# Last attention block prepares 512 tokens and computes four feed-forward units; the third chunk's transposes stand earlier; one barrier goes

## What is computed

```python
x = layernorm(x + attention(layernorm(x) * gamma + beta, w_qkv))
h = silu(x @ w1.T * s1) * (x @ w2.T * s2)            # 1024 wide
h = gelu(h @ h1.T * h1s); h = gelu(h @ h2.T * h2s)   # 1024 by 1024
out = layernorm(x + (h @ w3.T * s3))
```

## Time and profile before

| what | us |
|---|---|
| median of three runs | 2323.77 |
| the three runs | 2320.99, 2323.77, 2323.83 |
| the profiled execution | 2322.95 |
| its span | 2321.3 |
| TensorE busy | 2286.6 (99%) |
| VectorE busy | 1736.6 (75%) |
| ScalarE busy | 1607.4 (69%) |
| GpSimd busy | 204.5 (9%) |

### The profile page before, as it was taken

How to read it: one execution, slowest core, us unless ns; L and a number is a source line. 1 busy time by engine, 2 the same in 40 slices (tenths; PEclk the granted TensorE clock), 3 DMA queues, 4 the chain that set the end, 5 groups by cost and what they waited for, 6 DMA issues and landing times. The chain is left out here.

```text
span 2321.3 us, 40135 instructions
## 1 busy us (share of the span) xinstructions
PE 2286.6 (99%) x15394; PEld 1406.0 (61%) x15394; DVE 1736.6 (75%) x3755; ACT 1607.4 (69%) x3041; POOL 204.5 (9%) x236
## 2 busy tenths in 40 slices
PE   8999999999999999999999999999899999999998
PEld 4555555555555546555555555554588888888887
DVE  8999998988989887889888889894335544553543
ACT  4677887888989887889888899999523332332332
POOL 3211101011000101000010210001000000000000
PEclk8999999999999999999999999999999999999999
DMA  3110001100000210000021000205400000000000
GB/s 100 30 27 19 1 19 44 33 19 20 19 19 2 58 26 13 19 19 19 1 56 32 22 10 14 74 1 200 148 1 10 1 10 10 10 1 10 10 1 19
DMA packets 38995, 66.48 MB, mean 29 GB/s; under 512 B 9360, under 2 KB 19472, under 8 KB 37392
## 3 DMA queue, kind: packets, MB, share of 16 engines
q1 hardware_dynamic: 35136, 52.35, 8.3%
q0 software_dynamic: 3664, 11.53, 1.5%
HBM read 28.20 MB, written 4.19 MB: 14 GB/s over the span
## 5 line engine op out<-in xcount | busy, mean ns | idle before, releaser
L692 ACT ACTIVATE PR<-bank 128x512 f32<-128x512 f32 (+1 forms) x2176 | 1096.5, 591 | 74.9 <-PE bank L986 68.3
L781 DVE TENSOR_REDUCE pm<-bank 128x1 f32<-128x512 f32 x1471 | 944.0, 683 | 148.8 <-PE bank L960 128.0
L1003 PE MATMUL bank<-PR,V 128*17 128x512 f32 (+3 forms) x4608 | 554.1, 563 | 1.2 <-ACT PR L692 0.9
L1358 PE MATMUL bank<-e_hid,e_h_sb 128*128 128x512 f32 x2048 | 477.6, 395 | 0.0
L981 PE MATMUL bank<-MR,ones 64*128 64x512 f32 (+3 forms) x2304 | 462.9, 384 | 1.1 <-DVE pm L781 0.2
L1358 PEld LDWEIGHTS bank<-e_hid,e_h_sb 128*128 128x128 f32 x2048 | 385.1, 188 | 91.2
L1176 ACT ACTIVATE e_tmp<-bank,e_s_sb 128x512 f32<-128x512 f32 x128 | 88.3, 690 | 341.6 <-PE bank L1358 341.3
L981 PEld LDWEIGHTS bank<-MR,ones 64*128 64x128 f32 x2304 | 236.8, 185 | 72.4 <-ACT PR L692 35.6
L784 DVE CUSTOM_DVE_ANT_0 bank<-bank,below 128x256 f32<-128x256 f32 (+3 forms) x512 | 237.2, 520 | 26.6 <-PE bank L960 25.1
L1299 DVE CAST e_hid<-e_tmp 128x512 fp32r<-128x512 f32 x128 | 54.4, 425 | 258.3 <-ACT e_tmp L1176 258.3
L960 PE MATMUL bank<-KA,QX 64*128 64x512 f32 (+2 forms) x992 | 241.0, 441 | 3.3 <-ACT qk_sb L660 0.6
(11 more groups left out here) (121 smaller groups left out, 1751.2 us busy)
## 6 DMA issues: line engine op xcount, KB each, us to landing
xnT<-in_h_dram SPq DMA_DIRECT2D x8, 1024.0 KB, 5.0
e_h_sb<-in_h_dram POOLq DMA_DIRECT2D x2, 4096.0 KB, 19.9
KA<-qk_hi SPq DMA_DIRECT2D x88, 64.0 KB, 2.3
KA<-qk_lo SPq DMA_DIRECT2D x88, 64.0 KB, 2.2
QX<-qk_hi SPq DMA_DIRECT2D x80, 64.0 KB, 2.3
QX<-qk_lo SPq DMA_DIRECT2D x80, 64.0 KB, 2.3
xres<-in_x_dram SPq DMA_DIRECT2D x8, 512.0 KB, 8.2
out_dram<-e_y SPq DMA_DIRECT2D x7, 512.0 KB, 2.9
```

The lines of the kernel that those rows point to most:

```text
L692: act.activation(PR[:, s % NPB, h, off:QB], ring_bank("score", s, h)[:, off:QB], ACT.Exp).then_inc(exp_done, 1)
L781: dve.reduce_max(pm[:, B % 2, i, a, p, 1 + c:2 + c], bank[:, :], AX.X).then_inc(mx_done, 1)
L1003: last = pe.matmul(ACC[32 * h:32 * h + VW, q:QB], V[:, v_tile(B, tile), GH * (B // NJ % 2) + h, :], PR[:, s % NPB, h, at:at + QB - q], sta ...
L1358: last = pe.matmul(RING[(4 + n) % NR][:, :], w[:, c, P * o:P * (o + 1)], hid[:, (T + layer) % 2, part, c, :], start=(c == 0 and part == 0) ...
```

## The change

In the list of operations: the `norm` of chunk 2 moves ahead of `direct` (1, 2), `maxT` 0 and `direct` (1, 3). In the last block, after step 4 and ahead of the test, a new `x1` lets VectorE compute the statistics, the inverse deviation (by an integer start value and three Newton rounds, in place of ScalarE's root) and the normalised first 512 tokens. After the last scores a new `x1_turn` transposes them and VectorE writes the two parts. After the last block's sums are complete, a `first` unit (4 matmuls, one of the two products of a gate unit) is computed ahead of the accumulator's transposes, and three more after them. These four go to banks 0 to 3, where the feed-forward expects gate units 0 and 1, and its TensorE starts with unit 2. SyncE loads the scales ahead of the weight chunks of the test. ScalarE loads the table of Silu at the end of the attention. The barrier inside the exact branch goes. The first hidden matrix is loaded in two halves of its columns. The kept normalised copy of tile 0's tokens is made at the end of its gate units. The diff, cut to its core:

```diff
@@ -48,6 +48,9 @@
 DEVIATIONS = ((0, 1), (1, 3), (3, NJ))
 WARM = 5
 INTRO_UNITS = 6
+FIRST = 4
+ROOT_BITS = float(0x5F3759DF)
+NEWTON = 3
 COPIED = ("norm", "qk", "v", "maxT", "acc", "acc_copy")
@@ -140,9 +143,10 @@
                 self.ops.append(("av", s - 1))
             self.ops += after.get(s, []) + units[half:] + last.get(s, [])
             if (B, t) == (NB - 1, 4):
-                self.ops.append(("test",))
-        self.ops += [("av", len(STEPS) - 2), ("av", len(STEPS) - 1), ("acc_copy", NB - 1), ("acc", NB - 1),
-                     ("out", NB - 1)]
+                self.ops += [("x1",), ("test",)]
+        self.ops += [("x1_turn",), ("av", len(STEPS) - 2), ("av", len(STEPS) - 1), ("acc_copy", NB - 1),
+                     ("first", 0), ("acc", NB - 1), ("out", NB - 1)]
+        self.ops += [("first", n) for n in range(1, FIRST)]
@@ -181,7 +185,8 @@
 
         def take(use):
             nonlocal now
-            n = min(range(NRING), key=lambda n: back[n])
+            kept = {("acc", NB - 1): FIRST, ("x1_turn", 0): 2, ("x1_turn", 1): 2}.get(use, 0)
+            n = use[1] if use[0] == "first" else min(range(kept, NRING), key=lambda n: back[n])
             now = max(now, back[n] + 105)
             bank[use], former[use], holder[n], back[n] = n, holder[n], use, math.inf
@@ -216,11 +221,14 @@
             if op[0] == "av":
                 width = (QB - offset(*STEPS[op[1]])) / QB
                 now = max(now, ended[op[1]]) + 854 * width + 290
-            if op[0] == "norm":
+            if op[0] in ("norm", "x1_turn"):
                 for f in range(EC):
-                    n = take(("norm", op[1], f))
+                    n = take(op + (f,))
                     now += 440
                     by_scalar(n, now + 195, 730)
+            if op[0] == "first":
+                take(op)
+                now += 910
             if op[0] in LENGTHS:
@@ -240,8 +248,8 @@
                 ("inverse", 1), ("scale", 1), ("scale", 2), ("direct", 0, 0), ("direct", 0, 1), ("norm", 1),
                 ("direct", 0, 2), ("direct", 0, 3), ("stat", 3)]
         ops += first[:half] + [("direct", 1, 0)] + first[half:] + [("rowmax", 0), ("neg", 0)]
-        ops += [("stat", c) for c in range(4, NJ)] + [("direct", 1, 1), ("direct", 1, 2), ("maxT", 0), ("direct", 1, 3),
-                ("norm", 2), ("qk", 2), ("v", 0)] + second + [("inverse", 2)]
+        ops += [("stat", c) for c in range(4, NJ)] + [("direct", 1, 1), ("norm", 2), ("direct", 1, 2), ("maxT", 0),
+                ("direct", 1, 3), ("qk", 2), ("v", 0)] + second + [("inverse", 2)]
         inexact = nc.values_load(low_bits[0:1, 0:1], min_val=0, max_val=2 ** LOW_BITS - 1)
         with nc.If(inexact == 0):
-            nc.all_engine_barrier()
-            feed_forward_exact(nc, w1, s1, w2, s2, h1w, h1s, h2w, h2s, w3, s3, out, xres, ident, eps, banks,
-                               x1T, early, early_load)
+            feed_forward_exact(nc, h1w, h2w, out, xres, ident, eps, banks, x1T, early, early_load, x1_mean, x1_rstd,
+                               scales, w3_scale, first_done)
@@ -529,6 +550,10 @@
                     load_weights(B // NJ + 1)
             sp.wait_ge(v_ready, NU)
             sp.wait_ge(qk_ready, qk_count(NB - 1))
+            for v, scale in enumerate(ff_scales[0:4]):
+                sp.dma_start(scales[:, v, :], scale).then_inc(scale_load, 16)
+            sp.dma_start(w3_scale[:, :], ff_scales[4].rearrange("(o e) -> o e", o=1).broadcast_to([P, E]))\
+              .then_inc(scale_load, 16)
             for n, chunk in enumerate(weight_chunks()):
                 if n == 0:
@@ -538,6 +563,7 @@
                 sp.dma_start(chunks[n % 2], chunk).then_inc(chunk_load[n % 2], 16)
             sp.wait_ge(or_done, n_chunks + 2)
             sp.dma_start(low_row[:, :], low_part[:, :]).then_inc(row_load, 16)
+            sp.wait_ge(scale_load, 16 * 5)
             sp.wait_ge(hi_stacked, stack_count(NB - 1))
             sp.wait_ge(lo_stacked, stack_count(NB - 1))
             for g in range(2, G):
@@ -741,6 +767,7 @@
                     copy_acc(op[1])
                 if op[0] == "acc":
                     copy_sums(op[1])
+            act.activation(table[:, :], eps[:, :], ACT.Silu).then_inc(tabled, 1)
 
         @block.vector
         def _(dve):
...
+            def x1_statistics():
+                dve.wait_ge(res_done, NB - NJ + 1)
+                for i in range(TI):
+                    dve.bn_stats(stats[:, i, :], xres[:, i, :]).then_inc(x1_stat, 1)
+                dve.wait_ge(x1_stat, TI)
+                for i in range(TI):
+                    dve.bn_aggr(x1_mean[:, i, :], stats[:, i, :]).then_inc(x1_stat, 1)
+
+            def x1_inverse():
+
+                value, turn = std[:, 0, :, :], std[:, 1, :, :]
+                dve.wait_ge(x1_stat, 2 * TI)
+                dve.tensor_scalar(value, x1_mean[:, :, 1:2], EPS, None, ALU.add).then_inc(x1_root, 1)
+                dve.wait_ge(x1_root, 1)
+                dve.tensor_scalar(turn.bitcast(int32), value.bitcast(int32), 1, None, ALU.logical_shift_right)\
+                   .then_inc(x1_root, 1)
+                dve.wait_ge(x1_root, 2)
+                dve.tensor_scalar(x1_rstd[:, :, :].bitcast(int32), turn.bitcast(int32), -1.0, ROOT_BITS,
+                                  ALU.mult, ALU.add).then_inc(x1_root, 1)
+                for n in range(NEWTON):
+                    dve.wait_ge(x1_root, 3 * n + 3)
+                    dve.scalar_tensor_tensor(out=turn, in0=x1_rstd[:, :, :], scalar=-0.5, in1=x1_rstd[:, :, :],
+                                             op0=ALU.mult, op1=ALU.mult).then_inc(x1_root, 1)
+                    dve.wait_ge(x1_root, 3 * n + 4)
+                    dve.tensor_tensor(turn, turn, value, ALU.mult).then_inc(x1_root, 1)
+                    dve.wait_ge(x1_root, 3 * n + 5)
+                    dve.scalar_tensor_tensor(out=x1_rstd[:, :, :], in0=turn, scalar=1.5, in1=x1_rstd[:, :, :],
+                                             op0=ALU.add, op1=ALU.mult).then_inc(x1_root, 1)
+
+            def x1_normalise():
+                dve.wait_ge(x1_root, 3 * NEWTON + 3)
+                for i in range(TI):
+                    dve.tensor_scalar(xn_one[:, i, :], xres[:, i, :], x1_mean[:, i, 0:1], x1_rstd[:, i, :],
+                                      ALU.subtract, ALU.mult).then_inc(x1_done, 1)
+
+            def x1T_parts():
+                dve.wait_ge(st_ready, st_count(START[NB - 2] - 1, GH - 1))
+                for f in range(EC):
+                    dve.wait_ge(x1t_ready, f + 1)
+                    dve.tensor_copy(x1T[:, 0, f, :], ring_bank("x1_turn", f)[:, :]).then_inc(x1t_hi, 1)
+                    dve.wait_ge(x1t_hi, f + 1)
+                    dve.tensor_tensor(x1T[:, 1, f, :], ring_bank("x1_turn", f)[:, :], x1T[:, 0, f, :].bitcast(fp32),
+                                      ALU.subtract).then_inc(x1t_lo, 1)
 
             def test_weights():
@@ -868,6 +939,12 @@
                     invert_sums(op[1])
                 if op[0] == "test":
                     test_weights()
+                if op[0] == "x1":
+                    x1_statistics()
+                    x1_inverse()
+                    x1_normalise()
+                if op[0] == "x1_turn":
+                    x1T_parts()
 
         @block.tensor
...
@@ -1004,6 +1083,31 @@
                                          V[:, v_tile(B, tile), GH * (B // NJ % 2) + h, :],
                                          PR[:, s % NPB, h, at:at + QB - q], start=(t == 0), stop=(t == steps_of(B) - 1))
                 last.then_inc(av_done, 1)
+
+            def transpose_x1():
+                pe.wait_ge(x1_done, TI)
+                for f in range(EC):
+                    ring_free("x1_turn", f)
+                    for i in range(TI):
+                        last = pe.transpose(ring_bank("x1_turn", f)[:, P * i:P * (i + 1)],
+                                            xn_one[:, i, P * f:P * (f + 1)], ident[:, :])
+                    last.then_inc(x1t_ready, 1)
+
+            def first_unit(n):
+
+                o, at = divmod(n, 2)
+                w, loaded = early[at][0], early[at][2]
+                if n < 2:
+                    pe.wait_ge(loaded, 16)
+                for c in range(EC):
+                    if n == 0:
+                        pe.wait_ge(x1t_lo, c + 1)
+                    if c == 0:
+                        ring_free("first", n)
+                    for part in range(2):
+                        last = pe.matmul(ring_bank("first", n)[:, :], w[:, c, P * o:P * (o + 1)], x1T[:, part, c, :],
+                                         start=(c == 0 and part == 0), stop=(c == EC - 1 and part == 1))
+                last.then_inc(first_done, 1)
 
...
@@ -1127,13 +1229,14 @@
             @block.gpsimd
             def _(pool):
 
-                for dst, w, loaded in ((h1_sb, h1w, h_load[0]), (h2_sb, h2w, h_load[1])):
```

(37 more changed lines are left out.)

48 lines of the change are left out of this document (31 added, 17 removed).

## The result

| | before | after |
|---|---|---|
| median of the runs, us | 2323.17 | 2296.47 (2295.62 to 2297.0) |
| ratio, 95% interval | | 0.9886 [0.9874, 0.9898] |
| span of the profiled execution, us | 2321.3 | 2295.1 |

The account below looks back on a forecast made before the run. TensorE was taken to bound attention and feed-forward, leaving gains only at the seam and opening: 11.8 + 1.5 = 13.3 us off 2322.95 gives 2309.65, plus 0.8 for the median, hence 2310.4 us; range 2305 to 2316.

Parts of the forecast that it names:

- The seam: From last attention product to first hidden-layer matmul: hidden layer starts at 1654.7 instead of 1666.54, 11.8 us gained.
- the twelve matmuls: Three gate units after the accumulator transposes at the block's end: 2.7 us, hidden within 0.1 us.
- the string behind the transposes: ScalarE, VectorE and GpSimd work after the accumulator transposes, shifted 0.35 us; block's barrier moves from 1642.4 to about 1642.8.
- The copies out of a bank: VectorE making two parts of the transposed first tokens: two copies, two subtractions, 4 x 0.69 = 2.75 us, done at 1638.9.
- The lost barrier: Second barrier, at the exact branch, removed: it had let TensorE go at 1643.6 after 1643.3, priced at 0.3 us.
- The clock: TensorE at full clock through the seam, standing only about 1.1 us at the branch; the 1.8 us saved is within 11.8.
- The rival at half clock: Clock stays or falls to half at the branch: price 1.8 to 4.9 us, 2312.2 to 2315.3; chance 0.12.
- The weights: First half of the hidden weights lands at 1651 to 1652.7, 1 to 3 us ahead of its use.
- the rival: First half of the hidden weights late, being wanted 12 us sooner: up to 4.6 us, to 2315.0; chance 0.10.
- The opening: Third chunk's transposes moved ahead remove TensorE's 1.87 us stand before block 2's QK projection: 1.5 us gained, bounds -1.5 to 3.
- The bank order: Planner's bank order in the attention falls back into the same order within 15 uses: 0, between -3 and 3 us.
- Rival 4: Different bank order makes TensorE wait in all 544 attention steps: 27 us at 0.05 us a step, 2337; chance 0.03.

Follow-up runs that it names:

- f1: The kernel after with the barrier put back at the head of the exact branch: 2297.14 us, ratio 0.9887.
- f3: The kernel after without the four first gate units in the last attention block, so all 64 gate matmuls follow the branch: 2301.3 us, ratio 0.9908.
- f2: The kernel after with the first hidden matrix loaded in one piece instead of halves: 2300.52 us, ratio 0.9903.
- e3: The kernel before with only the new order of the opening: 2321.61 us against 2323.32.
- e4: The kernel after with the old order of the opening: 2299.28 us, 2.8 us above the kernel after.
- e1: The kernel before with 64 unused bytes per partition ahead of the hidden weights and what follows them: 2321.99 us against 2323.32.
- e5: The kernel before with 128 more unused bytes per partition ahead of the hidden activations: 2311.27 us against 2323.52.
- e6: The kernel after with 128 unused bytes per partition ahead of the hidden activations: 2307.87 us, ratio 0.9931.
- m2: Separate kernel without the layer: 128x512 matmuls, two weight tensors against sixteen moving tensors 32 bytes apart; 227.0 ns at distance 0, 234.3 at 160.
- g1: The kernel after with 96 unused bytes ahead of the hidden tensors, putting w3 at distance 192, hidden layer still 0: 2294.46 us, ratio 0.9878.
- g2: The kernel after with w3 at distance 192 and padding bringing the attention's large operands to distance 0: 2295.72 us, ratio 0.9880.
- m3: Separate kernel without the layer: sixteen moving tensors with 256-column matmuls (113.4 to 119.9 ns) and pairs on 64 rows (from 113.7 ns).

## Why the prediction was wrong, point by point

**The step that failed** is the first paragraph of the prediction: attention and feed-forward "both are untouched in the middle", "So the change can win only at that seam and in the opening". It put everything behind the first hidden matmul at nothing, and that stretch gave 12.8 us. The instructions were untouched; their operands' addresses were not. The whole diff showed it: scale tensors of 1152 bytes leave the place ahead of `hid` (these lines are not in the core of the diff above). And the trace of before showed a warning, since its own rows have gate matmuls at 14.54/64 = 0.227 us and hidden ones at 59.72/256 = 0.233, of one shape, both without idle time. I used 0.227 for the gates and never asked why the hidden layer was 2.7% slower (2.3% in the later tiles). That difference on 2048 matmuls was 11.3 us, and the `w3` matmuls added 1.5. No rival had it; the range ended at 2305.

**The rest of the sum** came to 13.4 us (11.1 and 2.3), for 13.3 forecast. The closeness is partly luck: the seam gave 0.7 less and the opening 0.8 more.

**The seam** was right in kind and 0.7 us too large (11.1 for 11.8). The barrier came 0.9 us later behind the last product, 0.4 were taken: the transposes of the accumulator are 0.7 us later instead of 0.35 (1.51 behind the last product instead of 0.81), and the twelve matmuls end last, at 1640.80. The prediction named them as the bound if the string behind the transposes were shorter; they took 3.00 us instead of 2.7, since 0.227 is the pace from start to start, and the last of a row ends some 0.3 later (12 x 0.227 = 2.7, measured 3.00). The 48 gate matmuls took 11.15 instead of 10.9, for the same reason. The copies out of a bank were 0.69 each, as taken (VectorE done at 1636.81). The lost barrier was worth 0.4 to 0.5 us (f1), where 0.3 stood.

**The clock** was right: full through the seam. TensorE stands 1.17 us at the branch, and the granted clock is 1.00 behind it. The rival at half clock did not come, but f3 shows its price where TensorE stands 3.67 us: 2.9 us. So it is the units in the block that save what half clock cost the seam before (1.8 us).

**The weights** were right: the half landed 8.6 us behind its issue at some 1642.1, at 1650.7, 2.4 us ahead of its use (1 to 3 were forecast). f2 shows that the rival was near: in one piece it is 2.9 us late. VectorE's subtractions beside the load did not starve it; it ran at 372 GB/s. The rule of the Trainium skill ("SBUF — State Buffer", section "SBUF: two separate sides") that was weighed there does not show in this trace either.

**The opening** was worth 2.3 us between the two traces, 1.7 by e3 and 2.8 by e4 in time, where 1.5 stood, within its bounds. The stand at QK is gone:

```profile
28.50 1.04 PE L988 MATMUL bank<-ident,PR 128*128 128x128 f32 x8
29.86 1.45 ACT L674 ACTIVATE xnT<-bank,gb 128x512 f32<-128x512 f32 x2
33.25 1.88 PE L1000 MATMUL bank<-xnT,wg 128*128 128x512 f32 x4
```

The copies by ScalarE end at 31.31, and the QK projection at 33.25 waits for nothing (compare). The place of the half-clock stretches in the opening differs between kernels, and the first attention product comes at 54.6 to 58.0 us. The mean granted clock of the first 70 us is 0.90 before and 0.93 after. e1 has the old order at 0.93 too, and its last attention product starts at 1638.00; the six traces with the new order at 0.93 have theirs at 1634.6 to 1636.0. So the order gains at an equal mean clock as well; how much of the 2.3 is from the removed stand, no run here tells.

**The bank order** was right at nothing: 0.6 us between before and after, within what traces of one order differ by. Rival 4 is out.

**What stays open.** That the distance sets the pace of the 128x512 form is shown by e5, e6 and the separate measurement (m2); why it does is not, nor what sets the pace of the form with 256 columns besides the distance (g1 against g2), nor whether the attention would gain from faster matmuls, since no padding tried made them faster.

## What to carry to other kernels

When a change adds, removes or resizes anything allocated ahead of a matmul's operands, work out the distance between its stationary and moving tensors modulo 256 bytes before and after, and price it by the count of matmuls; the best distance has to be measured for each form, and in place. In the profile, compare the time from start to start of like-shaped matmuls in different stages: two paces without idle time hint at a gain that may cost only some bytes of padding. At a seam, work that TensorE can do ahead of a barrier shortens its stand there, and that can be worth more than its own length: here a stand of 1.17 us kept the clock and one of 3.67 us lost 2.9 us (f3).

## What the runs showed of the hardware that was not expected

- A 128x512 fp32r matmul with its weight load takes 227.0 ns when stationary and moving operand lie 0 bytes apart modulo 256, 229.1 at 64, 234.3 at 160 and 233.3 elsewhere (m2, TensorE alone at work). With 256 columns it is 113.4 (192) to 119.9 ns (0); on pairs of 64 rows 113.7 (0) to 117.1 (m3). The best distance of one form is the worst of another.
- 128 bytes of padding moved this kernel by 12.2 us (e5) and 11.4 us (e6), 0.5%.
- The second barrier of all engines directly behind the first costs 0.4 to 0.5 us (f1). A 4 MB load in one piece took 13.8 us to land (f2; 15.3 in the kernel before), its half 8.6 (after).
